# Where a graph network's last weight product stands: behind its aggregation, or ahead of it in the layer before

## The reference, cut to what matters

```
h = maximum(layernorm(x), 0);  x = x + attention(h, adj, ...)                       # first layer
h = maximum(layernorm(x), 0);  x = x + relu((D^-1/2 adj D^-1/2 @ h) @ W + b)        # second layer
h = maximum(layernorm(x), 0);  x = x + relu(adj @ (maximum(sign(h),0) @ sign(w).T)) # third layer
h = maximum(layernorm(x), 0)                                                        # fourth layer
support = h @ weight
x = x + (1 - t) * support + t * (adj @ support)
```

## Time and profile before

| | us |
|---|---|
| median of 3 runs (1062.91 to 1066.08) | 1063.17 |
| profiled execution, own time | 1064.0 |
| its span | 1062.3 |
| layers 1, 2 and 3 start in it at about | 599.3, 794.5, 872.2 |
| TensorE busy | 1000.0 (94%) |
| VectorE, ScalarE busy | 751.9 (71%), 530.5 (50%) |

### The profile page before, as it was taken

One profiled execution on the slowest core, in us unless ns is written; L12 is line 12 of the kernel. 1 busy time (PEld: TensorE's weight loads), 2 busy tenths in 40 slices (PEclk: granted clock), 3 DMA queues, 4 the chain that ended last, 5 costly groups with the idle time before them and its releaser, 6 DMA issues.

```text
span 1062.3 us, 21121 instructions
## 1 busy us (share of the span) xinstructions
PE 1000.0 (94%) x7665; PEld 751.8 (71%) x7665; DVE 751.9 (71%) x1146; ACT 530.5 (50%) x874; POOL 84.4 (8%) x116
## 2 busy tenths in 40 slices
PE   8349989999999999999999979999999999999995
PEld 8338877888888888888888735555558884555553
DVE  4799898897797797797796545555656775555553
ACT  4667888888788788787776522222220000111110
POOL 1490000000000000000021000000002330000000
PEclk8569999999999999999999989999999999999998
DMA  5022444343343234244234014555455445666661
GB/s 225 11 81 87 125 123 130 96 114 123 85 122 123 83 119 128 80 122 128 80 117 151 31 63 174 181 192 176 170 173 192 155 160 167 213 212 212 212 212 59
DMA packets 36557, 143.73 MB, mean 135 GB/s; under 512 B 4236, under 2 KB 17701, under 8 KB 36389
## 3 DMA queue, kind: packets, MB, share of 16 engines
q1 hardware_dynamic: 35285, 142.37, 41.0%
q10 hardware_dynamic: 1232, 0.85, 0.3%
HBM read 128.72 MB, written 14.50 MB: 135 GB/s over the span
## 4 chain that ended last, share of the span: by engine, by line
PE 78%; DVE 6%; issue 4%; ACT 4%; POOL 0%; DVEq 0%; ACTq 0%; POOLq 0%
PE f_ya L1231 34%; PE f_ya L1154 17%; PE f_yb L1154 16%; PE f_yb L1138 8%; ACT f_gb L927 2%; DVE f_s_mat L1428 2%; DVE f_s_mat L1423 1%; PE f_yb L1132 1%; ACT f_s_mat L937 1%; PE f_ya L1132 1%; DVE f_wm L1415 1%; PE f_ya L1221 1%; DVE f_gb L1416 1%; DVE f_x_mat L1397 0%; PE f_ya L1214 0%
## 5 line engine op out<-in xcount | busy, mean ns | idle before, releaser
L1154 PE MATMUL f_ya<-f_x_mat,f_s_mat 128*128 128x257 f16 x2028 | 353.8, 273 | 29.1 <-DVE f_s_mat L1428 26.7
L1154 PE MATMUL f_yb<-f_x_mat,f_s_mat 128*128 128x257 f16 x2028 | 335.7, 274 | 0.0
L1231 PE MATMUL f_ya<-f_x_mat,f_a 128*128 128x512 f16 x1352 | 319.6, 382 | 3.5 <-DVE f_x_mat L1479 3.5
L1231 PEld LDWEIGHTS f_ya<-f_x_mat,f_a 128*128 128x128 fp8e4 x1352 | 132.1, 99 | 138.2 <-DVE f_x_mat L1479 4.0
L1154 PEld LDWEIGHTS f_yb<-f_x_mat,f_s_mat 128*128 128x128 f16 x2028 | 197.0, 97 | 29.7
L1154 PEld LDWEIGHTS f_ya<-f_x_mat,f_s_mat 128*128 128x128 f16 x2028 | 150.3, 97 | 49.1 <-issue 30.4
L927 ACT ACTIVATE f_gb<-f_e_tile,f_expc 128x256 f32<-128x256 f32 x338 | 140.4, 499 | 30.5 <-DVE f_s_mat L1428 24.7
L1423 DVE SCALAR_TENSOR_TENSOR f_s_mat<-f_wm,f_s_mat 128x1792 f16<-128x1792 f32 (+1 forms) x52 | 98.4, 1892 | 64.7 <-ACT f_s_mat L937 62.0
L1157 PE MATMUL f_ya<-f_ones,f_a 128*128 128x1 f16 x676 | 112.3, 166 | 0.0
L1537 DVE SCALAR_TENSOR_TENSOR f_gb<-f_gb 128x1664 f32<-128x1664 f32 x52 | 98.0, 1887 | 10.4 <-DVE f_s_mat L1587 10.4
L1415 DVE TENSOR_TENSOR f_wm<-f_gb,f_a 128x1792 f32<-128x1792 f32 (+1 forms) x52 | 98.1, 1886 | 1.8 <-issue 0.8
(11 more groups left out here) (137 smaller groups left out, 848.0 us busy)
## 6 DMA issues: line engine op xcount, KB each, us to landing
f_gb<-adj_dram SPq DMA_DIRECT2D x52, 832.0 KB, 4.8
f_a<-f_a_dram SPq DMA_DIRECT2D x39, 832.0 KB, 4.4
f_a<-adj_t_dram SPq DMA_DIRECT2D x26, 896.0 KB, 5.0
f_a<-adj_t_dram SPq DMA_DIRECT2D x26, 768.0 KB, 4.5
f_a_dram<-f_a SPq DMA_DIRECT2D x26, 224.0 KB, 5.2
f_a_dram<-f_a SPq DMA_DIRECT2D x26, 192.0 KB, 4.6
out_dram<-f_s_mat SPq DMA_DIRECT2D x25, 128.0 KB, 4.5
f_xs<-x_dram SPq DMA_DIRECT2D x3, 768.0 KB, 9.1
```

Of the source, the lines that this page charges most:

```text
L1154: return pe.matmul(bank[:, 0:F + 1], s_mat[:, j, side, i], x_mat[:, j, x_side, 0:F + 1], start=start, stop=stop)
L1231: return pe.matmul(bank_a[p][:, 0:W], a8_pair[:, r, at:at + P], x_layer[layer][:, j, 0:W], start=(j == 0), stop=(j == TILES - 1))
```

## The change

Layer 3's support `h @ weight` is made during layer 2, tile by tile, and layer 3 aggregates the support; x already holds `x + (1 - t) * support` when it starts. In layer 2, `norm` becomes one operation. TensorE transposes its result (f32) at block 20 two tiles later. ScalarE takes the relu into f16, VectorE the f16 rest. At block 6 of the next tile TensorE multiplies: three f16 products for each half of the features (high x high, high x low, low x high). ScalarE writes the high part of the support, VectorE the low part and the share of x. For tiles 23 to 25 this happens in the first pair of layer 3, where two blocks of each tile are now held. After a tile of layer 3 VectorE has two operations (`output`), and nothing follows on TensorE. Checks 25 to 28 stand behind the first two outputs. The weight is split into two f16 parts once, at the start of layer 1, and its range is flagged.

The diff, cut to its core:

```diff
-        EPILOGUE_AT = {1: (9, 15), 3: (13, 19)}
+        EPILOGUE_AT = (9, 15)
+        SUPPORT_AT = (6, 20)
 # SP
-                                store(t - 2, p)
+                                store(t - 1, 1 - p)
                     if layer == 3:
                         load_check(14, 1, CHECKS1 + 4)
+                        store(0, 0)
 # ScalarE, in place of layer 3's product and turned_copy
+                def pair2(k, first):
+                    for p in range(2):
+                        t = 2 * k + p
+                        a.wait_ge(zt_psum[3], t + 1)
+                        if not (first and p == 0):
+                            a.wait_ge(p_done[3], t)
                         settle()
+                        a.activation(yt16[:, 0, 0:F], ep[:, 0:F], ACT.Relu).then_inc(zt_done[3], 1)
+                        a.wait_ge(p_done[3], t + 1)
+                        settle()
+                        a.activation(x_layer[3][:, bass.ds(t, 1), 0:F], bank_b[p][:, 0:F].rearrange("p (a f) -> p a f", a=1),
+                                     ACT.Copy, scale=S3 / (WS * SCALE)).then_inc(x3_hi, 1)
 # TensorE
+                def support_turn(t, p, first=False):
+                    pe.wait_ge(nrm, t + 1)
+                    if not first:
+                        pe.wait_ge(zt_low, t)
+                    settle()
+                    for c in range(FB):
+                        tr = pe.transpose(ep[:, c * P:(c + 1) * P], ubuf[:, p, c * P:(c + 1) * P], ident[:])
+                    tr.then_inc(zt_psum[3], 1)
+                def support_project(t, p, first=False):
+                    if first:
+                        pe.wait_ge(w3_done, 2)
+                    pe.wait_ge(zt_low, t + 1)
+                    if not first:
+                        pe.wait_ge(sup_added, t - 1)
+                    settle()
+                    for c in range(FB):
+                        for y_part, w_part in ((0, 0), (0, 1), (1, 0)):
+                            mm = pe.matmul(bank_b[p][:, 0:F], yt16[:, y_part, c * P:(c + 1) * P], w3_16[:, w_part, c, :],
+                                           start=(c + y_part + w_part == 0), stop=(c == FB - 1 and y_part == 1))
+                    mm.then_inc(p_done[3], 1)
 # in tile()
+                            if layer == 2 and j == SUPPORT_AT[0] and not first:
+                                support_project(t - 3, 1 - p, second)
+                            if layer == 2 and j == SUPPORT_AT[1]:
+                                support_turn(t - 2, p, first)
 # in the first pair
-                    held = 1 if layer == 3 else 2
+                    held = 2
+                            if layer == 3 and (p, j) in ((0, 2), (0, 14), (1, 2)):
+                                back = {(0, 2): 3, (0, 14): 2, (1, 2): 1}[p, j]
+                                support_project(TILES - back, back % 2)
+                            if layer == 3 and (p, j) in ((0, 6), (0, 18)):
+                                support_turn(TILES - 2 + (j == 18), int(j == 18))
 # VectorE
+                    def output(t, p, k, first=False):
+                        xt = xs[:, bass.ds(t, 1), :].rearrange("p a f -> p (a f)")
+                        v.wait_ge(mm_done[3], t + 1)
...
+                        v.scalar_tensor_tensor(w_res[:], bank_a[p][:, F:2 * F], t_scaled[:], xt, ALU.mult, ALU.add)\
+                         .then_inc(sum3, 1)
...
+                        v.scalar_tensor_tensor(xo[:, p, :], bank_a[p][:, 0:F], t_scaled[:], w_res[:], ALU.mult, ALU.add)\
+                         .then_inc(z_done[3], 1)
 # norm
+                        v.tensor_scalar(ubuf[:, p:p + 1, :], xs[:, bass.ds(t, 1), :], mv[:, p, 0:1], cst[:, p:p + 1],
+                                        ALU.subtract, ALU.mult).then_inc(nrm, 1)
+                    def support_low(t):
+                        v.wait_ge(zt_done[3], t + 1)
+                        settle()
+                        v.scalar_tensor_tensor(yt16[:, 1, 0:F], ep[:, 0:F], 0.0, yt16[:, 0, 0:F], ALU.max, ALU.subtract)\
+                         .then_inc(zt_low, 1)
+                    def support(t, p):
...
+                        v.wait_ge(x3_hi, t + 1)
...
+                        v.scalar_tensor_tensor(xt, sup, omt_w[:], xt, ALU.mult, ALU.add).then_inc(sup_added, 1)
 # order of VectorE's work in a tile of layer 2: update(t), norm(t - 1), support(t - 2), support_low(t - 1)
 # order in layer 3
+                                output(t, p, k, first)
+                                if first and p == 1:
+                                    for n in range(4):
+                                        check(CHECKS1 + n, 1 - n % 2)
+                                if not first and not (last and p == 1):
+                                    check(CHECKS1 + 2 + t, 1 - p)
 # layer 1, behind check(0, 0)
+                        v.tensor_scalar(w3_16[:, 0], w_sb[3], WS, None, ALU.mult).then_inc(w3_done, 1)
+                        v.wait_ge(w3_done, 1)
+                        v.scalar_tensor_tensor(w3_16[:, 1], w_sb[3], WS, w3_16[:, 0], ALU.mult, ALU.subtract).then_inc(w3_done, 1)
+                        step(v.tensor_reduce(w_top[:, 0, :], w3_16[:, 0], AX.X, ALU.max))
+                        step(v.tensor_reduce(w_top[:, 1, :], w3_16[:, 0], AX.X, ALU.min))
...
```

More of the change, by code:

```diff
@@ L34 @@
 UP, DOWN = 64.0, 2048.0
+WS, S3 = 256.0, 16.0
+W_MAX, W_MIN = 15.0, 2.0 ** -6
 GROUPS = [(g, min(4, TILES - g)) for g in range(0, TILES, 4)]
@@ L825, in _ @@
                         pair(PAIRS - 2, r0 ^ 1, False)
-                        for t in range(TILES - 4, TILES):
+                        for t in range(TILES - 3, TILES):
                             store(t, t % 2, t == TILES - 1)
@@ L1033, in _ @@
                 x1_run(t + 2, t + 4)
[L1035 to L1046, removed]
-                        settle()
[L1048 to L1068, removed]
@@ new lines, in _ @@
+                in_pairs(a, pair1)
+                sign_product(TILES - 2)
+                turned_copy(TILES - 1)
+                sign_product(TILES - 1)
+                def pair2(k, first):
+                    for p in range(2):
+                        t = 2 * k + p
+                        a.wait_ge(zt_psum[3], t + 1)
+                        if not (first and p == 0):
+                            a.wait_ge(p_done[3], t)
+                        settle()
+                        a.activation(yt16[:, 0, 0:F], ep[:, 0:F], ACT.Relu).then_inc(zt_done[3], 1)
[3 more added lines that the diff above has]
+                                     ACT.Copy, scale=S3 / (WS * SCALE)).then_inc(x3_hi, 1)
@@ L1232, in block, with tile @@
                                          start=(j == 0), stop=(j == TILES - 1))
-                    def tile(q, p, r, n):
+                    def tile(q, p, r, n, first=False, second=False):
                         t = 2 * q + p
@@ L1280, in _ @@
                         mm.then_inc(mm_done[layer], 1)
[L1281 to L1284, removed]
+                    if layer == 1:
+                        second_epilogue(0, 0, 0)
+                        second_epilogue(0, 0, 1, True)
+                    tile(1, 0, r0 ^ 1, 16, True)
+                    tile(1, 1, r0 ^ 1, 16, False, True)
+                    tile(2, 0, r0, 32)
+                    tile(2, 1, r0, 32)
+                    with pe.Fori(1, PAIRS // 2) as k:
                         for i in range(2):
@@ L1606, in pair @@
                             t = 2 * k + p
[L1607 removed]
+                            if layer == 3 and last and p == 1:
                                 v.wait_ge(check_done, CHECKS)
                                 v.tensor_reduce(flags[:, 0:1], bad[:], AX.X, ALU.add).then_inc(flc, 1)
[L1610 to L1611 removed]
+                                v.wait_ge(flc, 9)
+                                v.tensor_reduce(flags[:, 4:5], flags[:, 0:4], AX.X, ALU.add).then_inc(flagd, 1)
                             if layer == 2:
+                                if last and p == 1:
+                                    norm(t - 1, 1 - p)
                                 update(t, p, k)
+                                if not (first and p == 0) and not (last and p == 1):
+                                    norm(t - 1, 1 - p)
+                                if not first:
+                                    support(t - 2, p)
                                 if not (first and p == 0):
[L1615 to L1619, removed]
[L1621 removed]
+                                    support_low(t - 1)
                             if layer == 1:
+                                update(t - 1, 1 - p, k if p else k - 1)
                                 product(t, p)
                                 check(t - 1, 1 - p)
[L1625 to L1626 removed]
+                            if layer == 3:
+                                output(t, p, k, first)
[4 more added lines that the diff above has]
+                                    check(CHECKS1 + 2 + t, 1 - p)
```

(18 more changed lines are left out.)

119 lines of the change are left out of this document (69 added, 50 removed).

## The result

The changed kernel has a median of 1069.35 us (15 runs, 1066.18 to 1071.05), the kernel before 1063.98 (15 runs, 1060.76 to 1066.39). The ratio is 1.0048, with a 95% interval of 1.0035 to 1.0061: slower by some 5 us (0.5%), where 7 less were forecast. The profiled execution took 1068.8 us with a span of 1067.1, 4.8 more than before (1064.0 and 1062.3). Of these 4.8, 1.7 lie ahead of layer 2, whose tile 2 starts at 805.74 instead of 804.05; over all profiles of this case layer 1 began anywhere between 598.1 and 602.8, whatever the kernel (599.3 and 601.0 in two profiles of the same kernel before). I count them as a difference between executions. From layer 2's tile 2 to the end the kernel before took 258.3 in this profile and 256.7 in its repeat (experiment 8), the changed one 261.4: 3.1 or 4.7 longer, against 5.4 in the medians.

The account below looks back on a forecast made before the run. TensorE was taken as the bound. Terms -27.7 - 4.1 + 20.2 + 1.8 + 2.4 + 0.25 + 3.2 + 1.0 - 3.45 gave -6.4: 1057.6 profiled, 1056.8 at the median's level; range 1051.5 to 1062.

Parts of the forecast that it names:

- Stores go out one tile earlier, behind the same load: nothing.: Layer 3's loop: stores issued one tile earlier, behind the same load, were to cost nothing.
- hand-off in layer 2: Layer 2: the product comes 0.08 us late on 22 tiles, +1.8; bounds 0 and 0.3 a tile (6.6).
- The queue behind the checks: Layer 3, before tile 4: late checks and loads on SP stop TensorE, +3.2; bounds 0 and 5.6.
- The landing at 22.3: Start of layer 3: the load of check 27 lands at U + 22.3, U being the stage's start.
- Clock after that stop: Layer 3, after the stop at tile 4: half clock costs 1.0 us, between 0 and 1.7.
- Rival (b): Stop at tile 4 with loads served side by side, half clock after: 1059.9, or 1062.5 with slower hand-off; chance 0.14.
- The pause "of about 4": Start of layer 3, kernel before: TensorE pause at 883 to 887, followed by half clock costing 1.7.
- the -27.7: Layer 3's 24 looped tiles: 162.34 us becomes 134.6 at 5.61 a tile, 1.7 of half clock included.
- Rival (a): Layer 2 bound by the hand-off, slower than before from 0.37 us a tile; 1066 at 0.5; chance 0.09.
- rival (d): Layer 3 becomes bound by its loads: at 230 GB/s a tile takes 6.13, time 1069; chance 0.07.
- the tail: After layer 3's last block: two VectorE operations, 1.3 us with waits instead of 4.75, -3.45.
- rival (c): No stop at tile 4 and no hand-off loss: 1050.8; chance 0.15.

Follow-up runs that it names:

- experiment 8: The kernel before, run again unchanged for one more profile, as a control: one run, 1062.8 us.
- experiment 1: Changed kernel with each store of layer 3 issued ahead of the check load beside it: 1062.87 us, 0.9989 of the kernel before.
- experiment 3: Changed kernel with layer 2's f16 product at block 10 instead of 6 of the next tile: 1064.78 us, 1.001 of the kernel before.
- experiment 4: Changed kernel with layer 2's f16 product at block 3 instead of 6 of the next tile: 1076.24 us, 1.0114 of the kernel before.
- experiment 5: Changed kernel with stores ahead of check loads, checks 25 and 26 ahead of output(0), f16 product at block 10: 1054.72 us, 0.9916 of the kernel before.
- experiment 6: As experiment 5, with tile 0's held blocks ahead of tile 1's block 16 in layer 3: 1053.14 us, 0.9905 of the kernel before.
- experiment 9: As experiment 6, with check 26 moved between output(0) and output(1): 1054.26 us, 0.9907 of the kernel before.
- experiment 10: As experiment 9, with layer 2's f16 product at block 8 instead of 10: 1053.35 us, 0.9901 of the kernel before.
- experiment 7: The kernel before with only checks 25 to 28 of layer 3 moved behind product(1) and update(0): 1070.51 us, 1.0063 of the kernel before.

## Why the prediction was wrong

The step that failed is the last sentence on layer 3: "Stores go out one tile earlier, behind the same load: nothing." A store stands behind a load that waits for a check, and in the new order that check is late. This step does not carry the whole miss: with the stores ahead (experiment 1) the time is 1062.87, still 0.9 above the range. The second step is the size of the hand-off in layer 2. In the profiles the forecast missed by 11.2 us (-6.4 against +4.8). By its steps:

- *The queue behind the checks, +3.2.* Issues, landings and the end of check 28 were right within 1.4 us (check 28 and output(2)'s start at 28.2 us into the stage instead of 26.9, pair 2 landing near 28.3 instead of 27.4). I followed two items of SP's list to their readers, check 28 and pair 2, and not the third, the store. It held output(2) some 3.5 longer: a stop of 6.49 (miss 3.3). Experiment 1 takes just this away and finds 2.96, so the rest of the stop was right. (The landing at 22.3 takes a load at 4.4 us, where the earlier trace rows have 4.6; it makes 0.2.)
- *Clock after that stop, +1.0.* It was 2.8: the last 22 tiles took 126.2 instead of 22 x 5.61 = 123.4 (miss 1.8). It is the stop's follower: the two other profiles with this stop of 6.5 (experiments 3 and 4) took 126.5 and 126.1 for the same tiles, and with 3.0 (experiment 1) nothing was lost. Rival (b) had the half clock, but for another reason. The pause "of about 4" from which the term was taken was misread: TensorE waited 2.00 and 0.56 there, with two transposes and four products in between, and half clock followed it in one of three profiles. The 1.7 in the -27.7 was thus of that execution.
- *Hand-off in layer 2, +1.8.* 4.4 (miss 2.6). I had 1.36 us against 1.30. Each hop was 0.03 to 0.09 longer than the row from layer 1's tail: 1.34, and 0.15 for the products after a wait. The stated bound (0.3 a tile) held it; the value was taken from the favourable end. Rival (a) would have had to cost 0.37 a tile; it was 0.19.
- *Stops not in the sum.* 0.82 at layer 2's first turn, which waits for the norm of tile 0 and so for GpSimd's scale: the moved work meets a start at which nothing is ahead. 0.95 before tile 2, which waits until output(0) has read its bank. They are the rest of the misses of layer 2 (3.5 in all) and of layer 3's start (1.0).
- *1.7 ahead of layer 2* are of the execution, as experiment 8 has it.

That the two profiles add up to the miss is a sum of one pair of executions; by the medians the miss is 12.6 (1056.8 against 1069.35), and the 1.4 more are not placed.

Right were: 5.61 us for a tile of layer 3 with nothing between the pieces; 0.65 for the six f16 products when they don't wait; no bound by the loads (rival (d): that its 1069 is the measured time is chance); VectorE and ScalarE keep up in layer 2; the weights' split hidden in layer 1, where VectorE still waits for TensorE behind it; and the tail (-3.7 for -3.45). So the moved work gains what was counted; the order around it gives it back. Experiments 5, 6, 9 and 10 show that: with the same work and other places it is 9 to 11 us faster than before.

The range, 1051.5 to 1062, took both ends of the stop from loads and checks alone, 0 and 5.6, and the clock from 0 to 1.7; it left no room for the stops that were not in the sum. (Its lower end stands above the 1050.8 that rival (c) itself gives.) Either step alone puts the time above it: 1062.87 with only the stores ahead (experiment 1), 1064.78 with only the product later (experiment 3). These two edits without that of the checks were not tried together.

Left open is what sends the clock down. The stop of 3.5 us before layer 1's held blocks was followed by half clock in all twelve profiles, those of 4.5 and 6.5 in the four that have them, and the one of 3.0, in one profile, was not; no run tried lengths between 3.0 and 3.5, and the pause at the start of layer 3 before went both ways.

## What to carry to other kernels

When an engine's program is reordered, walk every queue that waits for it to the end: each item behind the waiting one, loads and stores alike, and the buffer that each of them frees. A hand-off between engines that just fitted on paper was late here (1.36 forecast, 1.49 measured): leave a few tenths of a microsecond, which cost nothing where other blocks could stand in between. Edits that come together should be priced, and tried, one at a time: here one of them, alone, cost about what the whole change lost. And profile the kernel before twice before a term is read off one pause: one of the two profiles had 1.7 us of half clock that the other lacks.

## What the runs showed of the hardware

- *A small store behind loads was as slow as they.* The 128 KB store of tile 0 landed 6.80 us after its issue behind 832 KB loads (7.46 in experiment 1, behind three of them); the median over the changed kernel's 25 is 4.9, while its last, of 112 KB and with no load ahead, took 1.8. The Trainium skill, "DMA: Bandwidth & Descriptors", section on queues, rings and completion order, says that on each DMA engine descriptors are consumed in ring order. By that rule the store waits its turn whatever its size; these landings agree.
- *What a stop costs beyond itself.* In layer 3 the stops of 3.0 us (experiment 1) and under were followed by full clock (0.216 a block), those of 4.5 (experiment 7: six blocks in 2.40) and 6.5 (after) by half clock, 2.8 us more in the last case. A pause of about 4 with six short matmuls in it (before) was followed by half clock in one of three profiles (before and experiments 7 and 8). The Trainium skill, "TensorE: Matmul & The Clock Gate", section on HAM oscillation, warns of long waits for loads inside a stream of matmuls; the 6.5 us stop agrees, and the one of 3.0, with full clock behind it, shows that a wait can be too short for it.
- *The first matmuls after a wait.* Six f16 products take 0.65 in a running stream (0.66 at block 10), and 0.81 after a wait of even 0.03 us (at block 6).
